# A graph network on one core: the order of VectorE's work inside one step of the first edge pass

## The reference, cut to what matters

```
deg     = segment_sum(ones, dst);   agg_sum = segment_sum(x[src], dst)
hp      = relu(x @ W_pool + b_pool)
agg_max = segment_max(hp[src], dst)           # 0 where a node has no edge
out1 = BN(x @ W_self1 + agg_sum / max(deg, 1) @ W_neigh1)
out2 = BN(x @ W_self2 + agg_max @ W_neigh2)
x    = layernorm(x + leaky_relu(out1 + out2))
...                                           # layer 1: attention over the same edges
```

## Time and profile before

| | |
|---|---|
| time, median of 3 runs | 4267.63 us (4261.71 to 4274.33) |
| the profiled execution | 4270.08 us, span 4268.4 us |
| granted PE clock, mean | 0.989 of full speed |
| busy share of the span | PE 91%, PEld 79%, POOL 73%, DVE 62%, ACT 34% |
| first edge pass | from about 8 us to about 2050 us |
| second edge pass | from about 2200 us to about 4200 us |

### The profile page before, as it was taken

One profiled execution on the slowest core, in us unless ns is written; L12 is line 12 of the kernel. 1 busy time (PEld: TensorE's weight loads), 2 busy tenths in 40 slices (PEclk: granted clock), 3 DMA queues, 4 the chain that ended last, 5 costly groups with the idle time before them and its releaser, 6 DMA issues.

```text
span 4268.4 us, 114391 instructions
## 1 busy us (share of the span) xinstructions
PE 3889.0 (91%) x31146; PEld 3381.9 (79%) x31146; DVE 2637.0 (62%) x9276; ACT 1449.3 (34%) x3823; POOL 3118.9 (73%) x3252
## 2 busy tenths in 40 slices
PE   7888888888888888888899999999999999999996
PEld 5777777777777777777589999999999999999996
DVE  6665555565555555555556666666666666666666
ACT  3333333333333333333343333333333333333333
POOL 7777777777777777777157777777777777777774
PEclk9999999999999999999899999999999999999997
DMA  3111111111111111111134444444444344443442
GB/s 90 40 39 40 39 39 40 39 39 40 39 39 40 39 39 39 39 39 39 47 110 117 116 116 116 116 116 116 116 116 116 116 116 116 116 116 116 116 116 78
DMA packets 209079, 333.36 MB, mean 78 GB/s; under 512 B 73181, under 2 KB 156824, under 8 KB 208952
## 3 DMA queue, kind: packets, MB, share of 16 engines
q0 software_dynamic: 129040, 238.05, 21.8%
q1 hardware_dynamic: 80008, 94.94, 7.7%
HBM read 325.49 MB, written 7.24 MB: 78 GB/s over the span
## 4 chain that ended last, share of the span: by engine, by line
PE 59%; POOL 19%; issue 13%; DMA 6%; DVE 2%; POOLq 1%; ACT 0%; DVEq 0%; SPq 0%; ACTq 0%
POOL kvg L394 19%; PE bank L1143 10%; PE bank L1121 10%; PE bank L1129 10%; PE bank L1138 9%; PE bank L1160 8%; DMA kvg<-in_x_dram,idx 6%; PE bank L989 3%; PE bank L1000 2%; PE bank L1011 2%; PE bank L1028 2%; PE bank L1152 2%; PE bank L991 1%; PE bank L1069 1%; PE bank L1070 1%
## 5 line engine op out<-in xcount | busy, mean ns | idle before, releaser
L394 POOL DMA_INDIRECT kvg<-kv_table,idx x1613 | 1556.3, 965 | 510.0 <-issue 389.3
L394 POOL DMA_INDIRECT kvg<-in_x_dram,idx x1613 | 1534.8, 952 | 497.0 <-issue 456.8
L643 DVE TENSOR_SCALAR S<-iotaW,rel 128x64 f32<-128x64 f32 x4848 | 894.2, 272 | 26.4 <-issue 26.2
L989 PE MATMUL bank<-ident,kvg 128*96 128x128 f32 x3232 | 449.9, 282 | 313.7 <-DMA kvg<-in_x_dram,idx 299.7
L668 DVE TENSOR_TENSOR acc<-acc,bank 97x64 f32 (+1 forms) x808 | 177.5, 220 | 802.3 <-PE bank L1011 510.2
L989 PEld LDWEIGHTS bank<-ident,kvg 128*96 128x96 f32 x3232 | 364.1, 163 | 379.2 <-DMA kvg<-in_x_dram,idx 268.8
L551 ACT COPY eaC<-bank 96x512 f32<-96x512 f32 x404 | 235.1, 582 | 1120.2 <-PE bank L1121 1117.6
L467 ACT COPY eaC<-bank 96x512 f32<-96x512 f32 x404 | 235.2, 582 | 982.7 <-DVE scan L658 972.0
L892 DVE COPY qwin<-bank 64x96 f32<-64x96 f32 x404 | 100.9, 250 | 681.1 <-PE bank L1160 468.3
L658 DVE TENSOR_TENSOR_SCAN scan<-keepC,scan,bank 96x512 f32<-96x512 bf16 x404 | 512.2, 1268 | 0.0
L1028 PEld LDWEIGHTS bank<-S,scanE 128*96 128x96 f32 x3232 | 339.0, 165 | 216.8 <-issue 215.1
(11 more groups left out here) (125 smaller groups left out, 4804.2 us busy)
## 6 DMA issues: line engine op xcount, KB each, us to landing
ea<-in_edge_attr_dram SPq DMA_DIRECT2D x402, 192.0 KB
kvg<-in_x_dram,idx POOLq DMA_INDIRECT x1613, 2.5
kvg<-kv_table,idx POOLq DMA_INDIRECT x1613
kv_table<-stage SPq DMA_DIRECT2D x6, 672.0 KB, 3.3
stage<-counts_row SPq DMA_DIRECT2D x1, 2352.0 KB, 12.9
xN<-in_x_dram SPq DMA_DIRECT2D x6, 336.0 KB, 3.5
out_dram<-xN SPq DMA_DIRECT2D x6, 336.0 KB
src_all<-in_src_groups_dram SPq DMA_DIRECT2D x1, 804.0 KB
```

What stands on the lines that cost most here:

```text
L394: pool.indirect_dma_start(out=to[:, r, j, :], out_offset=None, in_=table, in_offset=bass.IndirectOffsetOnAxis(ap=idx[:, r, j:j + 1], axis= ...
L643: last = dve.tensor_scalar(S[:, r % R, n, :], iotaW[:, :], rel[:, bass.ds(i * R + r, 1), n // J, n % J:n % J + 1] .rearrange("p a b -> p ( ...
L989: pe.matmul(bank[0][0:D, j:GE:J], xg[:, r, j, 0:D], ident[:, :], start=True, stop=True)
```

## The change

In the DVE's step of the first pass, the running maximum of r-2 and the one-hot comparison of r move from behind the two accumulations to ahead of them, the running maximum first. The instructions, their operands, their waits and their numbers stay the same; no other engine's program changes.

```diff
                 for r in steps:
+                    if live(r - 2):
+                        running_max(r - 2)
+                    if live(r):
+                        one_hot(i, r, 2, s_max, s_S)
                     if live(r - 1):
                         features(i, r - 1)
                         add_window(r - 1, DSUM, 0, s_sum, s_acc)
                     if live(r - 4):
                         add_window(r - 4, D, 1, s_max, s_accm)
-                    if live(r):
-                        one_hot(i, r, 2, s_max, s_S)
-                    if live(r - 2):
-                        running_max(r - 2)
```

## The result

The change made the kernel slower: 4287.93 us (median of 5 runs, 4285.6 to 4288.56) against 4267.63 us, a ratio of 1.0049 with a 95% interval from 1.0039 to 1.0060. The forecast was 4267.6 us, no change.

A forecast was written before the change was run, and what follows sets the result against it. POOL's unbroken gathers, 1.25 us each and 5.00 us a group, were taken to bound the first pass. 4270.1 + 0 + 0 + 0 = 4270 us profiled, 4267.6 us against the median; range 4258 to 4280 us.

The forecast's parts named there:

- the bound and its cover: First pass: POOL issues gathers without a break, 5.00 us a group; earlier DVE results behind that gain nothing.
- DVE's new round: DVE's step in the first pass: 4.61 us at most, 4.7 us with the loop's turn, below POOL's 5.00 us.
- the first accumulation's register load: DVE, behind the eight comparisons: 0 to 0.79 us of idle time, taken as 0.79 us.
- The end of the pass: Drain after the last gather lands, 14.7 us without POOL: change taken as 0, with 1 us either way.
- The start: Steps 4 to 20 and unrolled turns: taken as 0, with a possible gain of 1.8 us from gathers no longer stretched.
- My nine stretched gathers: Unrolled turns before the change: nine gathers lengthened by 0.05 to 0.43 us, 1.8 us together.
- POOL's gathers beside the comparisons: Gathers running during DVE's comparisons: lengthening taken as 0; bounds 0.27 us a step (109 us) loss, 1.8 us gain.
- the band of the earlier trace: Loop before: comparisons start 0.22 us before to 0.19 us after a gather's start, and gathers stay at 0.95 us.
- Comparisons and gathers fall out of step: Rival: later scan at the loop's turn pushes comparisons past a gather's start; 27 us, 4295 us; chance 0.06.
- The rule that I weighed: Shared VectorE/GpSimd port: whoever comes second is fully blocked until the first is done; 4446 us, chance 0.01.
- the 178 us: Loss if a gather starting with the comparisons lasted to their end in every step: 404 x 0.44 us.

The follow-up runs named there:

- psum_numbers: Changed kernel, with the first pass's comparisons reading their numbers from PSUM instead of SBUF and ends moved to another bank: 4255.08 us, 0.9967 of the kernel before.
- old_order_pause: Order of before the change, with two 384-column copies from PSUM ahead of the comparisons: 4311.13 us, 1.0103 of the kernel before.
- scan_done: Changed kernel, with the comparisons waiting until the scan ahead of them has finished: 4261.86 us, 0.9983 of the kernel before.

## Why the prediction was wrong

**Right: the bound and its cover.** POOL paces the pass at four gathers a group, the loop gains nothing by earlier scans, and no wait of PE or DVE reached POOL. DVE's new round fits into the 5 us; the first accumulation's register load even hides mostly (1004.11 + 1.36 = 1005.47, accumulation at 1005.59 us), where I took 0.79 us. The end of the pass was worth nothing, as said, within the 1 us. The start was mis-sized: it gained 3.2 us, where I had 1.8 us at most. My nine stretched gathers left out one of 3.71 us at 33.72 us; the longest near there in the changed kernel, at 35.29 us, lasts 1.99 us.

**Wrong: the step "POOL's gathers beside the comparisons", taken as 0.** It had two parts. The first, that the comparisons keep the distance to the gather that the old loop showed: I had 0.07 us ahead of it; they start 0.18 us ahead on the mean, spread from 0.1 us behind to 0.5 us ahead, so about a third left the band of the earlier trace rows. The second, that inside this band a gather stays whole, is the one that failed. Inside the band 155 of 248 gathers beside the comparisons were stretched, outside it 53 of 130. At the distances of the table above it was 107 of 136 in the changed kernel and 1 of 97 before; more than 0.25 us ahead of the third comparison neither kernel has a stretched one. The band of the earlier trace rows was read from comparisons that come shortly after a stop of DVE, the register load's 0.62 to 0.79 us, with one accumulation of 0.22 us between the earlier trace rows. The change put the scan directly ahead of them, and what held in one neighbourhood didn't hold in the other. The term taken as 0 measured 21.6 us over the loop.

**The right rival, for half the reason.** "Comparisons and gathers fall out of step" stood there at 27 us for a step in four, with chance 0.06. The changed kernel has 208 steps at 0.11 us each, 23.0 us (over 0.945 us each); the other gathers are slightly shorter than before, which makes the loop's 21.6 us. Its condition, a scan that comes late where the loop turns, isn't what happened: by their place in the turn of four steps, 18, 81, 47 and 62 gathers are stretched, the fewest in the step where the loop turns.

**The rule that I weighed.** The Trainium skill, "SBUF — State Buffer", section "Who interferes with whom", names the shared port, and "VectorE: DVE Perf Modes", section "Why PSUM operands drop a tier", says that an operand in PSUM keeps VectorE out of the mode that takes both ports. psum_numbers is in line with both: 0 stretched gathers, and comparisons 1.60 us for 1.36 us; which mode the comparisons run in, no run shows. The first of these sections gives the lock for one instruction, and I had applied it to all eight comparisons as if they were one; hence the 178 us. The trace agrees with the narrower reading in so far as every stretched gather of the changed kernel ends within 0.03 us of a comparison's end, mostly the sixth or the seventh; in old_order_pause 225 of 237 end with the last. So a gather that ends amid comparisons was no evidence against the rule. I should have read the undisturbed rows as luck of the neighbourhood: the earlier trace rows together already had both outcomes.

What stays open is why comparisons that come shortly after a stop of DVE let most gathers through. Their own spacing doesn't show it: 0.163 us in the changed kernel and before, from the second comparison on.

## What to carry to other kernels

When POOL's gathers pace a stage, look at the duration of each gather and not only at waits: a reordering on DVE that costs no wait can lengthen them. Here they were comparisons that read and write SBUF on DVE, and moving their constant operand to PSUM freed the gathers even though the comparisons got longer (eight in 1.60 us for 1.36 us). A distance between two engines that was harmless in one order is no evidence for another order in which a different instruction runs ahead.

## What the runs showed of the hardware

A DVE instruction that has to wait for a semaphore of its own engine can make another engine faster: scan_done adds a wait and is 26 us faster than the changed kernel. A stretched gather ends with one of the comparisons, not at any time (in the changed kernel 1.08, 1.22, 1.38 or 1.54 us after their start), and the comparison that ends there lasts 0.28 us, or up to 0.47 us, instead of 0.25 us.
